# A gated delta-rule block with mixture of experts: spread order within a turn, the K convolution in the queries' memory, shared PSUM pairs, and two early gates

## The reference

```python
q, k, v = (silu(causal_conv(W @ h)) for each of q, k, v)      # 4 taps
k = k / max(norm(k), 1e-12);  alpha = sigmoid(Wa h + ba);  beta = sigmoid(Wb h + bb)
def step(S, xs):
    upd = vt - at * (S @ kt)
    S = clip(at * S + bt * outer(upd, kt), -5.0, 5.0)
    return S, S @ qt
g = silu(Wg h + bg)
out = (y * g) @ Wo.T
x = x + ga * out
```

## Time and profile before

| | |
|---|---|
| median of 3 runs | 2378.34 us (2376.22 to 2382.27) |
| profiled execution | 2367.01 us, span 2365.4 us |
| PE busy | 1924.9 us, 81% |
| weight loads (PEld) | 1379.2 us |
| DVE busy | 1489.1 us, 63% |
| ACT busy | 760.4 us, 32% |
| POOL busy | 1004.0 us, 42% |
| mean granted clock of PE | 0.816 |
| chain that ended last | DMA 9%, PE 4%, DVE 2% of the span |

### The profile page before, as it was taken

How to read it: one execution, slowest core, us unless ns; L and a number is a source line. 1 busy time by engine, 2 the same in 40 slices (tenths; PEclk the granted TensorE clock), 3 DMA queues, 4 the chain that set the end, 5 groups by cost and what they waited for, 6 DMA issues and landing times. The chain is left out here.

```text
span 2365.4 us, 59283 instructions
## 1 busy us (share of the span) xinstructions
PE 1924.9 (81%) x24750; PEld 1379.2 (58%) x24750; DVE 1489.1 (63%) x2181; ACT 760.4 (32%) x1250; POOL 1004.0 (42%) x1316
## 2 busy tenths in 40 slices
PE   6568889879888898888988889877389985999994
PEld 4245555646656566565565655656278884666653
DVE  5447567777686777766777767773478766444432
ACT  5223233333332333333333333331044433222221
POOL 0146264462552634716446255361154420455553
PEclk9679678797796877967878878785599986999997
DMA  3302111122111120220112201201543315344442
GB/s 112 76 1 59 46 32 46 35 64 56 35 50 52 38 62 29 64 62 29 46 37 63 56 28 47 64 23 35 185 170 116 116 38 198 91 87 85 87 84 44
DMA packets 89029, 156.52 MB, mean 66 GB/s; under 512 B 15676, under 2 KB 54084, under 8 KB 87564
## 3 DMA queue, kind: packets, MB, share of 16 engines
q1 hardware_dynamic: 72860, 124.76, 17.4%
q0 software_dynamic: 15904, 27.93, 6.1%
HBM read 112.53 MB, written 40.12 MB: 65 GB/s over the span
## 5 line engine op out<-in xcount | busy, mean ns | idle before, releaser
L976 PE MATMUL d_ps<-hT,d_w 128*128 128x512 f32 x768 | 414.4, 659 | 16.3 <-DMA d_cw<-convp_in 11.9
L703 POOL TENSOR_TENSOR d_ktok<-d_ktok,decay_tok 128x512 f32<-128x512 f32 x64 | 95.6, 1523 | 510.0 <-DVE d_kmax L840 487.3
L676 POOL TENSOR_TENSOR d_TT<-d_TT,d_tmp 128x31 f32<-128x31 f32 (+15 forms) x496 | 284.0, 573 | 38.9
L671 POOL TENSOR_TENSOR d_tmp<-d_Tq,d_TT 128x31 f32<-128x31 f32 (+15 forms) x496 | 262.8, 530 | 73.8 <-DVE d_TT L834 36.2
L976 PEld LDWEIGHTS d_ps<-hT,d_w 128*128 128x128 f32 x768 | 138.4, 206 | 121.0 <-issue 89.7
L1157 PE MATMUL d_ps<-d_Vp,d_XTz 64*64 64x64 f32 x2048 | 143.2, 261 | 65.3 <-DVE d_S L750 64.3
L569 ACT ACTIVATE d_U<-d_ps 128x128 f32<-128x128 f32 x256 | 70.2, 274 | 383.1 <-PE d_ps L1165 379.8
L750 DVE SCALAR_TENSOR_TENSOR d_S<-d_S,gamma_chunk,d_ps 128x64 f32<-128x64 f32 x448 | 106.9, 291 | 135.2 <-PE d_ps L1174 135.1
L1157 PEld LDWEIGHTS d_ps<-d_Vp,d_XTz 64*64 64x64 f32 x2048 | 111.1, 163 | 125.0 <-issue 124.7
L2043 POOL DMA_INDIRECT out<-m_yo,m_slot_i x71 | 112.7, 1587 | 131.6 <-DVE m_yo L2143 86.2
L1784 POOL TENSOR_TENSOR y<-y,g_sb 128x512 f32<-128x512 f32 x64 | 102.5, 1632 | 124.2 <-ACT g_sb L1768 123.6
(11 more groups left out here) (229 smaller groups left out, 4027.1 us busy)
## 6 DMA issues: line engine op xcount, KB each, us to landing
...
y_scratch<-d_yT SPq DMA_DIRECT2D x256, 64.0 KB, 2.0
d_arow<-ab_scratch SPq DMA_DIRECT2D x128, 128.0 KB, 3.0
...
```

The lines of the kernel that those rows point to most:

```text
L671: nc.gpsimd.tensor_tensor(tv, Tq[:, s + 1:, s].rearrange("p (r a) -> p r a", a=1).broadcast_to([P, left, known]), X[:, s, 0:known].rearran ...
L676: nc.gpsimd.tensor_tensor(X[:, s + 1:, 0:known], X[:, s + 1:, 0:known], tv, ALU.subtract).then_inc(s_sub, 1)
L976: return nc.tensor.matmul(dst[:, g, :], w[:, m % 2, n, dc, :], hT[:, dc, at:at + G], start=(dc == 0), stop=(dc == DC - 1))
```

## The change

It has two parts.

**The order of a turn.** The places of many operations in the 16 steps change, on PE, ACT and DVE; their number does not. The fixed alternation of the PSUM pairs is replaced by a free assignment, with the waits that belong to it, and K's convolution is done in `qT`, the queries' memory, which by then is free, and no longer in `TT` and `Tq`:

```diff
-RING = 20
-(AT_KK0, AT_KK1, AT_Q0, AT_Q1, AT_KT0, AT_V0, AT_KT1, AT_KQ0, AT_V1, AT_Z0,
- AT_KQ1, AT_P, AT_Z1, AT_X, AT_VT0, AT_VT1, AT_K0, AT_K1, AT_WA, AT_WB) = range(RING)
+(AT_KK0, AT_Q0, AT_V0, AT_KT0, AT_Z0, AT_KQ1, AT_P, AT_X, AT_K0, AT_WA, AT_WB,) = (0,) * 11
+(AT_KK1, AT_Q1, AT_KQ0, AT_KT1, AT_V1, AT_Z1, AT_VT0, AT_VT1, AT_K1,) = (1,) * 9
...
         def conv_dst(n, b2):
-            return (qT[:, b2, :], k_made[b2], v_made)[n]
+            return (qT[:, b2, :], qT[:, b2, :], v_made)[n]
...
             def first_k(u, b2):
                 act.wait_ge(s_w[u // BP % 2], 32 * (u // BP // 2 + 1))
                 act.wait_ge(s_kproj, 2 * u + b2 + 1)
-                act.wait_ge(s_x2, u)
+                act.wait_ge(s_kq, 2 * u)
+                act.wait_ge(s_qg, u)
...
                     pe.wait_ge(s_ksilu, 2 * u + 2)
                     if h == 0:
                         if it >= 1:
-                            pe.wait_ge(s_wt, 2 * it - 1)
+                            pe.wait_ge(s_wt, 2 * it)
...
                 if i == 0:
                     pe.wait_ge(s_xn, u + 1)
-                    if it >= 2:
-                        pe.wait_ge(s_mx, 2 * it - 3)
-                    else:
-                        pe.wait_ge(s_A, 2 * it + 1)
+                    pe.wait_ge(s_A, 2 * it + 2)
```

**Two gates in the last turn.** The gates of the groups 0 and 1 (`EARLY = 2`, 16 pieces) are made in iteration it = 16, in which there is a chain and no preparation, and the last two pieces in iteration 17:

```diff
+                    if it == TURNS and c >= 2:
+                        gate(c - 2, 0)
...
                     if chain and c < NCW - 1:
                         state_sum(tc, c)
+                    if it == TURNS and c >= 2:
+                        gate(c - 2, 1)
+                    if it == TURNS + 1 and c in (2, 6):
+                        gate(NCW - 2 + c // 4, 0)
+                        gate(NCW - 2 + c // 4, 1)
```

The verdict is no longer a part of its own. DVE compares in the last turn's block, PE multiplies the result by the identity, DVE reduces and casts:

```diff
+            nc.vector.tensor_scalar(bad[:], bad[:], 0.5, None, ALU.is_lt).then_inc(s_mx, 1)
+            split_input(3)
+            dve.wait_ge(s_zp, 2 * TURNS + 1)
+            nc.vector.tensor_reduce(fmax[0:1, :], ps[0:1, 4, 0:P], AX_X, ALU.max).then_inc(s_mx, 1)
...
+            nc.tensor.matmul(ps[0:4, 4, 0:P], bad[:], ident[:], start=True, stop=True).then_inc(s_zp, 1)
...
-            nc.gpsimd.partition_all_reduce(bad_all[:], bad[:], P, bass.bass_isa.ReduceOp.max).then_inc(s_g, 1)
```

`attn_out` loads y of group 0 first, then only the output weights; POOL takes the gates of the groups 0 and 1 from the kept ones, PE makes gates from group 2 on, and x has three buffers instead of four:

```diff
+XHOLD = 3
...
-            sp.dma_start(wg_sb, wg).then_inc(s_w, 16)
+            load_y(0)
             sp.dma_start(wo_sb, wo).then_inc(s_w, 16)
-            sp.dma_start(bg_sb[:], bg).then_inc(s_l, 16)
-            load_y(0)
...
-                    nc.gpsimd.tensor_tensor(y[:, g % 2, m, :], y[:, g % 2, m, :], g_sb[:, i % 4, :],
+                    nc.gpsimd.tensor_tensor(y[:, g % 2, m, :], y[:, g % 2, m, :],
+                                            gate_kept[g][:, m, :] if g < EARLY else g_sb[:, i % 4, :],
                                             ALU.mult).then_inc(s_m, 1)
...
             for g in range(NG + 3):
-                if g < NG:
+                if EARLY <= g < NG:
                     gate(g)
```

More of the change, by code:

```diff
@@ L660, in _ @@
                         keep_w(u, 1)
+            for i in range(NCW - 3, EARLY * M):
+                keep_gate(i)
         @block.gpsimd
@@ L1630, in _ @@
                 nc.vector.tensor_copy(r[:], u[:]).then_inc(s_y, 1)
-def high(nc, dst, src):
-    return nc.vector.tensor_copy(dst.bitcast(F32R), src)
-def low(nc, dst, src, hi):
-    return nc.vector.tensor_tensor(dst.bitcast(F32R), src, hi, ALU.subtract)
-def three(nc, dst, lhs, rhs, first, last):
-    for n, (a, b) in enumerate(((0, 0), (0, 1), (1, 0))):
-        ins = nc.tensor.matmul(dst, lhs(a).bitcast(F32R), rhs(b).bitcast(F32R),
-                               start=first and n == 0, stop=last and n == 2)
-    return ins
 SLOT_TILES = 71
@@ L1823, in _ @@
             nc.vector.memset(eps[:], LN_EPS).then_inc(s_ag, 1)
[L1824 to L1828 removed]
+            dve.wait_ge(s_w, 48)
+            halves([wo_s[:, a] for a in range(2)], wo_sb, s_ws)
             for g in range(NG):
```

579 lines of the change are left out of this document (338 added, 241 removed).

## The result

The changed kernel takes 2349.96 us (median of 4 runs, 2344.39 to 2353.78), the kernel before 2377.28 us (4 runs, 2370.57 to 2382.27): a ratio of 0.9894, 95% interval 0.9873 to 0.9915, 27 us less. Forecast were 2366 us, 12 us less. Measured a second time beside the experiments, the changed kernel stood at 0.9920 (0.9901 to 0.9940), 2354.66 against 2375.11 us, 20 us less.

What follows compares the result with a forecast made beforehand. Bound: a turn's cycle, POOL's substitution then a chained tail, with PE's low clock part of it. Order +3, last turn +2, verdict -4, ramp and first product -13 us: -12 us, 2366 us from a 2378.3 median; range 2330 to 2402.

Steps and rivals of the forecast that it cites:

- Only the tail counts: Only the 52.4 us from POOL's last substitution step to the next L819 set a turn's length; work under the substitution is free.
- (a): Tail start: X is transposed first, but Z's second half, waiting for POOL, precedes the first cross product: nothing gained.
- (b): Cross product halved by a chain step: second half ends 1.6 us later, ACT copy partly hidden, +0.4 us at second copy.
- (c): K maximum (2.28 us) moved ahead of the taps on DVE, hidden but for some 0.5 us: taps end +0.4 us.
- (d): Tail: the first kept U no longer waits 0.48 us for a DVE maximum; first state sum 0.4 us earlier.
- (f): Tail: y's transposition (1.30 us) follows the state update; second decay scan -0.4 us, fourth KK product +0.2: -0.2 us.
- (e): Tail: first KK product (1.91 us) waits for both W copies, behind the first state sum; timeline reaches a state update at 1436.8.
- Rival (2): KK behind both W copies keeps the clock low and work end to end: +2.3 us a turn, 2398 us; chance 0.16.
- Rival (1): The order removes a low-clock stretch of PE: turns 2.5 us shorter, 53 us less in all, 2325 us; chance 0.12.
- The last turn, +2 us: Two gates' products added to the last turn's steps, nearly offset by a higher clock: +2 us, between 0 and +33.
- Verdict -4: Between last maximum and new block, the verdict by a product and one DVE reduction replaces POOL's 8.6 us: -4 us.
- ramp -15.6: From new block to first output product, 42.6 us before: y rows load first, POOL multiplies at once, 27 us: -15.6 us.

Runs made afterwards that it cites:

- before_kk: The kernel before with only the first KK product moved behind the first state sum: 1.0283 of the kernel before, 67 us slower.
- undo_kk: The changed kernel with the first KK product back ahead of the first state sum: 2368.66 us, 0.9971 of the kernel before.
- order_only: The kernel before with the new turn order, PSUM pairs and K convolution memory, without gates, new verdict or output stage: 0.9965 of the kernel before.

## Why the prediction was wrong

The measured time lies in the range, but the gain is about twice the forecast, and two errors of opposite sign hide in it.

- **Between L819 and the substitution's end POOL is last: right** (44.0 us after L905; product at 47.9). **"Only the tail counts": incomplete.** `before_kk` shows the head growing by 2.1 us as soon as the chain is late in step 4.
- **(a) right. (b) and (c) +0.4 us: measured 0**; the second copy ends at 60.8 us in both kernels.
- **(d) to (f), -0.2 us: measured -0.8. This is the step that failed**, and with it the sum of +0.2 us a turn. The first update came 0.9 us earlier, where (d) gave 0.4 that (c) took back: KK's 1.9 us ahead of the sum were replaced by the y pieces of step 14, 1.2 us, which the timeline of (e) left out. That KK's place is needed is shown by `undo_kk` (12 to 18 us lost), that the y pieces are its partner is read from the listings and not shown. Rival (2) had KK's place as the loss. It is one in the kernel before: 67 us in `before_kk`.
- **The clock.** The prediction kept the low stretches, and for this change that was right: over the 15 turns the mean granted clock is 0.79 before and in `order_only`, and 0.81 and 0.79 in the two profiles of the changed kernel. Their place and length it had wrong: in the kernel before the long one begins in a pause of 2.1 us, not behind the one of 5, and the two together are some 40 us of a turn, not 23. With the pauses filled PE ran at 0.91 in the mean, most turns kept a single low stretch of about 10 us, and the time fell by 2%. That agrees with the rule of the Trainium skill (TensorE: Matmul & The Clock Gate, section HAM oscillation) that running without the pause keeps the clock high. Rival (1) had this mechanism, and 53 us for it; the order alone did not set it off, the fillings did.
- **The last turn, +2 us: measured +12.9, the other term that failed.** The clock rose from 0.50 to 0.83 over 1610 to 1660 us, but half a gate piece took 0.96 us at the high and 1.65 us at the low clock, not 0.75 and 1.5, and at the low clock halves, y pieces and the bound's scan all stood in the chain of the last two steps. The prediction had no price for these together. Run apart, they gave 10 us back in the trace.
- **Verdict -4, ramp -15.6: right** (-4.0, -16.0).
- **The 11 us between the profiled execution and the median** were taken as a constant. Turns at another clock are the likely reason, since two profiles of the changed kernel differ by 10 us in their turns; for the kernel before, of which there is one profile, it is not shown.

By the runs, the order is worth -9 us (forecast +3) and the gates -9 (forecast -15). The forecast's direction was right by luck in part: its gain was to come from the gates alone, and half of it comes from an order that was to cost a little.
